# GpSimd's additions of the pairs' products, cut into four instructions of 128 columns each

## The reference

```python
logits = xt @ Wr + br                                  # 8 experts
top_p, top_idx = jax.lax.top_k(softmax(logits), 2)
weights = top_p / top_p.sum(axis=-1, keepdims=True)
xe = xn[None] * ln_g[:, None, :] + ln_b[:, None, :]    # per expert
h = gelu(einsum('end,edh->enh', xe, W1) + b1[:, None, :])   # hidden width 256
y = einsum('enh,ehd->end', h, W2) + b2[:, None, :]
out = (weights[:, :, None] * chosen_two(y)).sum(axis=1)
```

## Time and profile before

| | us |
|---|---|
| median of 3 runs | 62.23 (62.0 to 62.38) |
| profiled execution, its own time | 62.09 |
| profiled execution, span of the core | 60.2 |

### The profile page before, as it was taken

One profiled execution on the slowest core, in us unless ns is written; L12 is line 12 of the kernel. 1 busy time (PEld: TensorE's weight loads), 2 busy tenths in 40 slices (PEclk: granted clock), 3 DMA queues, 4 the chain that ended last, 5 costly groups with the idle time before them and its releaser, 6 DMA issues.

```text
span 60.2 us, 1140 instructions
## 1 busy us (share of the span) xinstructions
PE 54.2 (90%) x332; PEld 31.2 (52%) x332; DVE 33.5 (56%) x154; ACT 33.7 (56%) x78; POOL 24.7 (41%) x48
## 2 busy tenths in 40 slices
PE   1998999799969999999999997999999999599830
PEld 0323667585847586872551674284462762232720
DVE  2279679458898959833900004799870000953920
ACT  5401568996996477959297179518749396000000
POOL 5157493000463399407329500299526000049400
PEclk9999999999999999999999999999999999999997
DMA  0451549760000000000000165510000037662011
GB/s 0 110 97 25 132 112 327 261 255 0 5 0 0 0 5 11 0 0 0 0 0 11 46 211 200 210 45 1 0 0 0 11 110 203 210 171 91 0 44 44
DMA packets 4309, 4.43 MB, mean 74 GB/s; under 512 B 2188, under 2 KB 2896, under 8 KB 4304
## 3 DMA queue, kind: packets, MB, share of 16 engines
q1 hardware_dynamic: 3984, 4.34, 24.0%
q10 hardware_dynamic: 320, 0.03, 0.5%
HBM read 4.08 MB, written 0.29 MB: 73 GB/s over the span
## 4 chain that ended last, share of the span: by engine, by line
PE 78%; DVE 8%; issue 3%; DMA 3%; ACT 1%; POOL 1%; ACTq 0%; POOLq 0%
PE banks L892 27%; PE banks L917 25%; PE banks L848 7%; PE banks L821 4%; PE banks L802 4%; DMA X<-in_x_dram 3%; PE banks L786 3%; PE banks L870 2%; PE banks L810 2%; DVE gated L662 1%; PE banks L861 1%; POOL rs L287 1%; PE banks L955 1%; PE banks L933 1%; DVE X L508 1%
## 5 line engine op out<-in xcount | busy, mean ns | idle before, releaser
L428 ACT ACTIVATE H<-banks,PF 128x512 f32<-128x512 f32 x32 | 20.0, 683 | 9.3 <-PE banks L892 9.3
L892 PE MATMUL banks<-XE,W1F 64*128 64x256 f32 x128 | 16.8, 395 | 0.0
L917 PE MATMUL banks<-H,W2F 128*64 128x512 f32 x64 | 15.3, 602 | 1.0 <-issue 1.0
L892 PEld LDWEIGHTS banks<-XE,W1F 64*128 64x128 f32 x128 | 11.6, 186 | 6.2 <-issue 5.2
L323 POOL TENSOR_TENSOR acc<-acc,gated 128x512 f32<-128x512 f32 (+1 forms) x6 | 6.5, 1089 | 14.3 <-DVE gated L662 14.1
L309 POOL TENSOR_SCALAR XE<-XF,PF,LB 128x256 f32<-128x256 f32 x15 | 8.3, 564 | 4.1 <-ACT XF L409 4.1
L662 DVE SCALAR_TENSOR_TENSOR acc<-banks,B2T,GS 128x512 f32<-128x512 f32 x2 | 1.5, 751 | 12.8 <-DMA GS<-gates_kept 12.8
L917 PEld LDWEIGHTS banks<-H,W2F 128*64 128x64 f32 x64 | 4.3, 136 | 8.4 <-issue 8.3
L293 POOL TENSOR_TENSOR rs<-base,half 128x4 f32<-128x4 f32 x4 | 4.1, 1028 | 9.6 <-DVE base L571 9.6
L786 PE MATMUL banks<-zeros 128*128 128x512 f16 x17 | 6.4, 497 | 1.3 <-POOL zeros L326 1.3
L662 DVE SCALAR_TENSOR_TENSOR gated<-banks,B2T,GS 128x512 f32<-128x512 f32 (+1 forms) x7 | 4.6, 670 | 2.3 <-PE banks L917 1.6
(11 more groups left out here) (81 smaller groups left out, 62.0 us busy)
## 6 DMA issues: line engine op xcount, KB each, us to landing
GS<-gates_kept SPq DMA_DIRECT2D x16, 128.0 KB, 2.9
W1F<-in_w_dram SPq DMA_DIRECT2D x1, 768.0 KB, 4.9
W2F<-in_w_dram SPq DMA_DIRECT2D x1, 512.0 KB, 4.7
W1F<-in_w_dram SPq DMA_DIRECT2D x1, 256.0 KB, 3.2
out_dram<-res SPq DMA_DIRECT2D x4, 64.0 KB, 2.0
X<-in_x_dram SPq DMA_DIRECT2D x2, 64.0 KB, 1.9
X<-in_x_dram SPq DMA_DIRECT2D x1, 128.0 KB, 2.6
WQK<-in_attn_w_dram ACTq DMA_DIRECT2D x2, 16.0 KB, 2.3
```

Of the source, the lines that this page charges most:

```text
L428: nc.scalar.activation(H[:, r, :].rearrange("p (t n) -> p t n", t=PT), ps_z[g // J % 2][:, :, PIX * j:PIX * j + PIX], ACT.Gelu, bias=PF[:, ...
L892: nc.tensor.matmul(ps_z[q % 2][:, k, PIX * j:PIX * j + PIX], W1F[rows, e, j, :], XE[h][rows, e, :], start=True, stop=True).then_inc(z_read ...
L917: mm = nc.tensor.matmul(ps_y[s % 2][C * k:C * k + C, :], W2F[:, u, :], H[:, (2 * J * s + J * k + j) % RING, :], start=(j == 0), stop=(j == ...
```

## The change

Every call of `add_up` issues four additions of 128 columns, in place of one of 512 (s = 1, 2, 3, 5) or two of 256 (s = 6). The semaphore is raised once per call as before, with the last part, and for s = 6 also with the second part, so that every count keeps its meaning: 5 stands for columns 0 to 255 of the last addition, 6 for all of it. GpSimd issues 20 additions where it issued 6. Nothing else differs.

```diff
-                cuts = 2 if s == STEPS - 2 else 1
-                for k in range(cuts):
-                    cols = slice(TOK // cuts * k, TOK // cuts * (k + 1))
-                    nc.gpsimd.tensor_tensor(acc[h][:, cols], acc[h][:, cols], gated[s % 2][:, cols], ALU.add)\
-                        .then_inc(acc_ready, 1)
+                for k in range(TILES):
+                    cols = slice(P * k, P * k + P)
+                    last = nc.gpsimd.tensor_tensor(acc[h][:, cols], acc[h][:, cols], gated[s % 2][:, cols], ALU.add)
+                    if k == TILES - 1 or (s == STEPS - 2 and k == IMG - 1):
+                        last.then_inc(acc_ready, 1)
```

## The result

| | before | changed |
|---|---|---|
| median (lowest to highest), 15 runs each | 62.19 (61.86 to 63.45) us | 62.98 (62.34 to 64.01) us |
| ratio of the times | | 1.0096, 95% interval 1.0063 to 1.0129 |
| profiled execution | 62.09 us, span 60.2 | 63.08 us, span 61.0 |

The ratio is +0.60 us of 62.19, between +0.39 and +0.80. The forecast was +0.34 us, and the 62.98 us lie at the upper edge of what it had left open (62.2 to 62.95), 0.03 us outside by the median and inside by the ratio (62.23 x 1.0096 = 62.83).

What follows compares the result with a forecast made beforehand. TensorE was taken to bound 39 to 51 us, and VectorE's chain through weigh(7) and L670 the end. GpSimd's longer end adds 0.34: 62.09 + 0.34 = 62.43 us profiled, 62.57 us median; range 62.2 to 62.95.

Steps and rivals of the forecast that it cites:

- The path moved to GpSimd: At the end, L670 waits for GpSimd instead of weigh(7): +0.34 us; a 0.5 us hole ahead of L943 costs nothing more.
- The price of a part: A 128-column GpSimd addition takes 454 ns; parts follow every 407 ns, so four last 1,675 ns.
- the fixed share: 182 ns of each GpSimd addition do not depend on its width; each column adds 2.125 ns.
- The slower rival: Parts in add_up(5) and add_up(6) do not overlap: 62.85 us without gaps (12%), 63.75 with 0.15 us gaps (6% for more).
- The sum: Whole kernel: 62.09 + 0.34 = 62.43 us profiled, 62.57 us for a median, +0.5%; 64% within 0.15 us.
- the step behind GpSimd: At the end, L670 starts 0.03 us after GpSimd's last part, as L508 follows L287: 56.99 us in place of 56.65.
- The slack as a fixed number: At the end, add_up(5) starts at 53.46 us as before; weigh(7) starts at 55.74, so 0.6 us hide its +0.41.
- The middle: add_up(1), add_up(2) and add_up(3) each last 0.41 us longer, hidden; 2.4 us cover add_up(3) before fold_sum; cost nothing.
- the gain: In the middle, VectorE runs 1.5 to 1.9 us earlier until 44 us; L643 ends at 42.2 to 42.6, not 44.09.
- The step that failed: In the middle, L599 waits some 0.4 us, L629 precedes add_up(2) or waits one part: together 1.5 to 1.9 us earlier.
- the cover: In the middle, TensorE's queue takes the gates at L901, 44.89 us, 0.8 us after they are ready, so nothing is gained.

Runs made afterwards that it cites:

- the reordered kernels: TensorE's turn_gates(1) ahead of layer1(13), ScalarE's copy ahead of gelu(24), against the kernel before: 0.9971, 0.9979; with middle parts 0.9884, 0.9966; with all parts 0.9943.

## Why the prediction was right, and where not

**The path moved to GpSimd: right.** L670 waits for GpSimd, there is a hole of 0.59 us ahead of L943 (0.5 forecast), and neither the hole nor the output transfers cost more than L670 does.

**The price of a part: right.** 454 ns forecast from the three other widths, 457 measured; eight parts of 64 columns confirm the fixed share. The slower rival, parts without overlap, did not occur: four parts last 1.70 us, less than 4 x 0.457, and start 0.41 us apart, as forecast. The time alone would have pointed to it: its 62.85 us lie nearer to the measured 62.83 (the ratio applied to 62.23) than the forecast of 62.57, whose band of 0.15 us was missed. Only the trace tells the two apart.

**The sum: too small, by the step behind GpSimd.** From `add_up(5)` to the last L690 the forecast was 58.16 - 53.46 = 4.70 us; the four profiles with both additions in four parts gave 4.80 or 4.81, so the term was +0.45 and not +0.34. Of the missing 0.11 us, 0.07 is the step from GpSimd's end to L670: I had taken 0.03 us from L287 and L508, and it is 0.10 (57.31 to 57.41); why the two places differ stays open. The rest is the parts themselves, 3.54 us for both additions against 3.50: each follows the one ahead after 0.413 us, not 0.407. The measured +0.60 (0.39 to 0.80) and +0.28 (-0.04 to +0.59) both contain 0.45.

**The slack as a fixed number: a gap in the prediction.** I took the start of `add_up(5)` as given. Over the fourteen profiles it lies 2.00 to 2.60 us ahead of `weigh(7)`, and the two leads of 2.00 us are those of profiles in which the gates of `weigh(5)` landed late. The uncut end absorbed that; the cut one passes it on. This is shown by stretches of four profiles, and it explains the 2.80 us tail with the end alone in parts. It does not explain anything in the changed kernel's own two profiles, where the lead was 2.3 us, as in both of the kernel before. That it explains the rest of the measured +0.60 is therefore argued, not shown; the later start of the full clock, in both profiles of the changed kernel, is as good a candidate, and neither is settled.

**The middle: nothing on the path, right; the gain, wrong.** I had the gates 1.5 to 1.9 us earlier; it was 0.25. The step that failed added the two waits of L599 and L629 and stopped there. Up to L621 the gain was 1.31 us; then VectorE's later instructions, moved forward into `add_up(2)`, paid 1.06 us of it for the parts, one after another. The Trainium skill's rule ("SBUF — State Buffer", "Practical consequences") would have told it, if applied to every VectorE instruction with two SBUF inputs in the stretch rather than to the two that were seen waiting: L621, L636 and L643 are of this kind, and the trace agrees with 0.73, 0.72 and 0.38 us where they took 0.29, 0.29 and 0.19 undisturbed in the kernel before. (It does not agree everywhere: in the first half L599 took 0.19 us inside GpSimd's L293, from 22.18 to 22.37 us within 21.56 to 22.57.) That the cover was TensorE's queue was right: in the reordered kernels the hole closes when the turn comes earlier, and parts in the middle still add nothing that shows.

## What to carry to other kernels

Before cutting an instruction that is hidden, measure its distance to the path at each instruction that waits for it, and multiply the fixed cost of an instruction by the cuts that stand in a row there; here 0.36 us of slack ahead of L670 met 0.7 us of fixed cost. Look also at whether the slack is the same in several profiles. Cut where the other engine is really held up and its result leads to the end, and leave the rest whole: in this kernel no addition met both conditions. When runs scatter by more than the effect, compare stretches between two instructions of the profile: 4.80 or 4.81 us came back four times while the spans of the same profiles lay between 60.8 and 61.4 us.

## What the runs showed of the hardware

- A small VectorE addition with both inputs in SBUF waits for the end of the GpSimd addition in progress, and gets in between two GpSimd instructions even though their records overlap by 0.04 us: L599 took 1.27 us beside one of 512 columns, 0.45 beside parts of 128; L629, a `tensor_scalar` with one input in SBUF, was held in the same way (1.23 us against 0.16). But in the first half of the kernel L599 took 0.19 us in the midst of GpSimd's L293, a power of 128x4 elements that lasts 1.01 us: it isn't held by every GpSimd instruction for its whole length.
- A float32 addition on GpSimd costs 316, 457, 726 and 1,270 ns for 64, 128, 256 and 512 columns, and consecutive ones start 0.04 us before the record of the one ahead ends.
- VectorE's L670 started 0.10 us after the end of the GpSimd addition that it waited for, in every profile where it waited for one; L508, at the start of the kernel, followed GpSimd's L287 by 0.03 us.
- The same matmuls on zeros (L786) took 631 or 634 ns each ahead of the record of the full granted clock and 379 behind it. That record begins anywhere from 4.34 to 7.31 us in fourteen executions, and `layer2(3)` started up to 0.9 us later where it began late.
- A transfer of the gates (L271) took 2.8 to 3.6 us from issue to landing at the same place in the program (the second for `weigh(5)`); where `weigh(5)` waited for it, it started 0.08 us after the landing.
